# Sorting the edges of a graph layer in 50 chunks of 2,000 with one scatter each, instead of 40 chunks of 2,500 with two scatters per pair

## The reference

```python
def _L0_gnn_ref(input, edge_index, edge_attr, W_weight, W_bias):
    support = jnp.einsum('ni,oi->no', input, W_weight) + W_bias
    row, col = (edge_index[0], edge_index[1])
    messages = support[col] * edge_attr[:, None]
    output = jax.ops.segment_sum(messages, row, num_segments=N_NODES)
    return output

edge_index = jnp.stack([src, dst])
x = x + _L0_gnn_ref(_layernorm(x, axis=-1), edge_index, edge_weight, ...)
x = x + _L0_ffn_ref(_layernorm(x, axis=-1)[None], ...)[0]
```

## Time and profile before

| | |
|---|---|
| median of 3 runs | 1578.63 us (1577.52 to 1581.45) |
| profiled execution: its own time | 1581.09 us |
| profiled execution: span | 1579.2 us |
| mean granted TensorE clock | 0.942 |
| front and ranks, until the first build | 0 to 131.9 us |
| portion A, until its records are loaded back | 131.9 to 246.4 us |
| stage B, first gather to first record load | 252.8 to 588.2 us |
| records loaded and unpacked | 588.2 to 605.5 us |
| stage C | 605.5 to 1265 us |
| last LSTM steps and output | 1265 to 1579.2 us |

### The profile page before, as it was taken

How to read it: one execution, slowest core, us unless ns; L and a number is a source line. 1 busy time by engine, 2 the same in 40 slices (tenths; PEclk the granted TensorE clock), 3 DMA queues, 4 the chain that set the end, 5 groups by cost and what they waited for, 6 DMA issues and landing times.

```text
span 1579.2 us, 36191 instructions
## 1 busy us (share of the span) xinstructions
PE 1373.5 (87%) x9451; PEld 1222.1 (77%) x9451; DVE 1317.3 (83%) x4072; ACT 637.6 (40%) x2150; POOL 1028.1 (65%) x1087
## 2 busy tenths in 40 slices
PE   5688784787777876999999999999999999999990
PEld 2557783566666753899999999999999989999990
DVE  8899977999999977888888888888888655666765
ACT  0626560000000000444444444444444577777770
POOL 0325546777777777777777777777777300888883
PEclk9799886999999987999999999999999999999995
DMA  9211112333433333444444444444444343344435
GB/s 228 63 53 41 31 12 66 97 85 89 142 87 97 86 92 100 132 136 151 149 139 156 131 156 125 158 130 156 137 148 153 113 142 119 120 124 125 119 92 164
DMA packets 60867, 183.27 MB, mean 116 GB/s; under 512 B 20474, under 2 KB 22050, under 8 KB 59810
## 3 DMA queue, kind: packets, MB, share of 16 engines
q0 software_dynamic: 41312, 98.34, 22.6%
q1 hardware_dynamic: 19500, 84.30, 16.7%
HBM read 141.25 MB, written 41.17 MB: 116 GB/s over the span
## 4 chain that ended last, share of the span: by engine, by line
PE 59%; DVE 13%; issue 7%; DVEq 2%; DMA 1%; ACT 1%; POOL 1%; ACTq 0%; POOLq 0%; SPq 0%
PE bank L2020 14%; PE bank L1970 13%; PE bank L2007 10%; PE bank L2014 10%; PE bank L1922 5%; PE bank L1885 3%; DVE big_a L1233 3%; DVE big_a L1228 1%; PE bank L1980 1%; DVE big_b L1483 1%; PE bank L1989 1%; DVE big_a L1699 1%; DVE big_b L1290 1%; DVE big_c L1284 1%; PE bank L2050 1%
## 5 line engine op out<-in xcount | busy, mean ns | idle before, releaser
L633 POOL DMA_INDIRECT big_a<-support_scratch,stg_g x510 | 488.5, 958 | 159.8 <-issue 138.1
L1970 PE MATMUL bank<-big_a,big_c 128*125 128x256 f32 x1020 | 303.6, 389 | 11.1 <-DVE big_c L1567 4.3
L586 POOL DMA_INDIRECT big_a<-support_scratch,stg_g x224 | 214.3, 957 | 75.4 <-issue 56.6
L2020 PE MATMUL bank<-big_c 128*128 128x125 f32 x2048 | 256.9, 280 | 5.2 <-DVE big_c L1455 3.9
L2020 PEld LDWEIGHTS bank<-big_c 128*128 128x128 f32 x2048 | 241.3, 191 | 16.0 <-issue 7.2
L1483 DVE TENSOR_TENSOR big_b<-big_b,bank 125x256 f32 x510 | 212.2, 416 | 22.7 <-PE bank L1970 21.1
L1567 DVE TENSOR_SCALAR big_c<-consts_sb,listed 128x125 f32<-128x125 f32 x510 | 182.8, 359 | 55.5 <-PE bank L1970 46.7
L2007 PEld LDWEIGHTS bank<-xt,w_ih 128*128 128x128 f32 x1600 | 209.0, 192 | 11.3 <-ACT xt L696 0.7
L2014 PEld LDWEIGHTS bank<-big_c 128*128 128x128 f32 x1600 | 208.9, 191 | 11.2 <-ACT bank L810 0.7
L2014 PE MATMUL bank<-big_c 128*128 128x125 f32 x1600 | 209.9, 275 | 0.0
L2007 PE MATMUL bank<-xt,w_ih 128*128 128x125 f32 x1600 | 209.5, 274 | 0.5 <-ACT xt L696 0.5
(11 more groups left out here) (308 smaller groups left out, 2309.7 us busy)
## 6 DMA issues: line engine op xcount, KB each, us to landing
big_c<-gate_input_scratch SPq DMA_DIRECT2D x64, 508.0 KB, 3.5
gate_input_scratch<-pr SPq DMA_DIRECT2D x25, 1016.0 KB
big_a<-support_scratch,stg_g POOLq DMA_INDIRECT x734
support_scratch<-pr SPq DMA_DIRECT2D x12, 448.0 KB
big_b<-in_x SPq DMA_DIRECT2D x2, 1904.0 KB
out<-big_a SPq DMA_DIRECT2D x2, 1456.0 KB
big_b<-in_x SPq DMA_DIRECT2D x1, 1792.0 KB
out<-big_a SPq DMA_DIRECT2D x1, 1344.0 KB
```

The source lines that it names most:

```text
L586: pool.indirect_dma_start(out=ring[:, s, :], out_offset=None, in_=sup_d, in_offset=bass.IndirectOffsetOnAxis(ap=stg_g[:, q, j:j + 1], axis ...
L633: pool.indirect_dma_start(out=ring[:, s, :], out_offset=None, in_=sup_d, in_offset=bass.IndirectOffsetOnAxis(ap=stg_g[:, r, n:n + 1], axis ...
L1970: mm(bank[4 + POSITION[n] % PSR][0:SEGS, 0:D], oneh[:, s % HELD, 0:SEGS], ring[:, s, :], start=True, stop=True).then_inc(prod, 1)
L2020: return mm(home, w_hh[:, k, g:g + P], h_s[:, q, k, :], start=False, stop=True, skip_group_check=True)
```

## The change

A chunk is now 16 columns (2,000 edges), 50 chunks, and each has a bank and a scatter of its own: 128 blocks at most, so one group, 32 columns instead of 64 in the one-hots, 64 columns of records instead of 128. PE moves these 64 columns twice in each product (a broadcast), so that a product still moves 128 columns and writes 128 columns of PSUM, of which the first 64 are used. There are again 800 products in all (50 times 16). Portion A has 18 chunks, stage B has 232 tiles and 32 chunks; `RUN` stays 510. In portion A ACT makes the slot one-hots of every third chunk. In stage B the hardware loops are gone: the program is written out, with a chunk after every 7 tiles (`SPACING`). The masks of the front are made in 11 pieces instead of 8. Supports are spread as 25 and 3 (`RANKING, MID`) instead of 20 and 8. `rows_of_blocks` handles 5 chunks at a time, ten times, with half the elements; five of these calls fall in portion A and five in B.

```diff
-CC = 20
+CC = 16
 CHUNKS = EC // CC
-PORTIONS = (14, 26)
+PORTIONS = (18, 32)
-GRP = 2
-NPOS = GRP * BLK
-SOON, FORE, RANKING, MID = 7, 14, 20, 8
+SOON, FORE, RANKING, MID = 7, 14, 25, 3
+SPACING = 7
...
+        def chunk_at(t):
+            return t // SPACING if t % SPACING == 0 and t // SPACING < PORTIONS[1] else None
+
+        def by_scalar(k):
+            return k < K0 and k % 3 == 2
...
-            def add_blocks(m, q, rows):
-                pool.wait_ge(evac, m + 3)
-                if not isinstance(m, int) or m > 0:
-                    pool.wait_ge(scat, scattered(m))
-                pool.sem_inc(go, 1)
-                for g in range(GRP):
-                    pool.indirect_dma_start(
-                        out=rec_d, out_offset=bass.IndirectOffsetOnAxis(ap=rows(g), axis=0),
-                        in_=stg_r[:, q, g, :], in_offset=None, compute_op=ALU.add).then_inc(scat, 16)
+            def add_blocks(k, rows):
+                pool.wait_ge(evac, k + 3)
+                if k > 0:
+                    pool.wait_ge(scat, scattered(k))
+                pool.indirect_dma_start(
+                    out=rec_d, out_offset=bass.IndirectOffsetOnAxis(ap=rows, axis=0),
+                    in_=stg_r[:, k % 2, :], in_offset=None, compute_op=ALU.add).then_inc(scat, 16)
...
-            with pool.Fori(1, whole) as it:
-                for q in range(2):
-                    gather_half(0, it * 2 + q, q, HALF)
-                second_portion(it + (M0 - 1))
-            gather_half(0, whole * 2, 0, HALF)
-            second_portion(whole + M0 - 1)
-            gather_half(0, whole * 2 + 1, 1, TIL[0] - whole * RING - HALF)
+            for t in range(TIL[0]):
+                gather(t)
+                i = chunk_at(t + 1)
+                if i is not None and i >= 3:
+                    second_portion(K0 + i - 3)
+            for i in range((TIL[0]) // SPACING - 2 if TIL[0] // SPACING < PORTIONS[1] else PORTIONS[1] - 3, PORTIONS[1]):
+                second_portion(K0 + i)
             load_records(1)
...
-                V.tensor_tensor(col_h, c.broadcast_to([EP, CC, NPOS]), several(iota[0:EP, 0:NPOS], CC), ALU.is_equal
+                V.tensor_tensor(col_h, c.broadcast_to([EP, CC, BLK]), several(iota[0:EP, 0:BLK], CC), ALU.is_equal
...
-            for m in range(M0):
-                if m + 1 < M0:
-                    build(2 * m + 2, 0)
-                if m == SIDE - 2:
-                    rows_of_blocks(1)
-                copy_records(m)
-                if m + 1 < M0:
-                    build(2 * m + 3, 1)
+            for k in range(K0):
+                if k + 2 < K0:
+                    build(k + 2)
+                if k in ROWS_IN_A:
+                    rows_of_blocks(ROWS_IN_A[k])
+                copy_records(k)
...
                 for c in range(CC):
-                    ins = mm(bank[b][:, 0:2 * NPOS], slots_home(k, q)[:, c, :],
-                             col_v[:, q, c, :, :].rearrange("p v n -> p (v n)"),
-                             start=q == 0 and c == 0, stop=q == 1 and c == CC - 1)
+                    once = col_v[:, k % 2, c, :, :].rearrange("p (o v) n -> p o (v n)", o=1)
+                    ins = mm(bank[b][:, 0:4 * BLK].rearrange("p (o n) -> p o n", o=2), slots_home(k)[:, c, :],
+                             once.broadcast_to([EP, 2, 2 * BLK]), start=c == 0, stop=c == CC - 1)
```

More of the change, by code:

```diff
@@ L792, in _ @@
-            stage_rows(whole + M0 - 1)
-            act.wait_ge(prod, whole * RING + RING)
-            stage_gather(whole * RING + HALF, 1, TIL[0] - whole * RING - HALF)
+            for i in range(2):
+                stage_values(K0 + i)
+            act.wait_ge(where_r, SIDE)
+            for t in range(1, TIL[0]):
+                if t % HALF == 0 and t // HALF >= 2:
+                    stage_half(t // HALF)
+                i = chunk_at(t)
+                if i is not None:
+                    if i + 1 < PORTIONS[1] and i >= 1:
+                        stage_values(K0 + i + 1)
+                    if i >= 2:
+                        copy_records(K0 + i - 2)
+                        stage_rows(K0 + i - 2)
@@ L796, in take_input @@
+            for i in range(PORTIONS[1] - 2, PORTIONS[1]):
+                copy_records(K0 + i)
+                stage_rows(K0 + i)
             def take_input(j, q, x, free=None):
@@ L1315, in _ @@
             unpack_all(0)
-            for i in range(2, SUPERS // SIDE):
-                spread_blocks(i)
             dve.wait_ge(small_r, 1)
@@ L1336, in _ @@
                 onehot(t, t)
[L1337 to L1357 removed]
+            for t in range(TIL[0]):
+                i = chunk_at(t)
+                if i is not None:
+                    build(K0 + i)
+                    if i in ROWS_IN_B:
+                        spread_blocks(ROWS_IN_B[i])
+                        rows_of_blocks(ROWS_IN_B[i])
+                if t % HALF == 0:
+                    vals = blocks(t, HALF)
+                if t + AHEAD < TIL[0]:
+                    onehot(t + AHEAD, t + AHEAD)
+                add_tile(t, t, acc[0:SEGS, ds(vals[t % HALF], D)])
             def row_of_place(j):
```

368 lines of the change are left out of this document (152 added, 216 removed).

## The result

| | us |
|---|---|
| before, 4 runs | median 1579.25 (1577.52 to 1581.45) |
| after, 4 runs | median 1593.28 (1592.61 to 1599.71) |
| ratio after / before | 1.0087, 95% interval 1.0067 to 1.0108 |
| forecast | 1594.6, range 1583 to 1609 |

The kernel is slower by 0.87 per cent, 14 us. The profiled execution of after has a span of 1590.8 us, 11.6 more than that of before, and a granted clock of 0.94.

A forecast was written before the change was run, and what follows sets the result against it. POOL and DVE were both taken to bound stage B, PE stage C, and chains between engines portion A's later stretch. Front 0, portion A -12 and stage B +28 gave +16 us, taken to the median: 1594.6 us, range 1583 to 1609.

The forecast's parts named there:

- The bound of stage B after: Stage B: POOL (GpSimd) sets the pace at 10.8 us per chunk of 7 gathers and a scatter; chance 0.78.
- The size of stage B: Stage B: 232 gathers, 29 scatters and 3 chained scatters sum to 362.0 us against 335.4; +28 taken, bounds +26.6 and +34.
- the allowance of 1.4 us for waits on top: Stage B: +28 taken where +26.6 held without any wait inside the stage, expecting fewer waits than the 3.6 us before.
- POOL and DVE are both bounds of stage B: Stage B before the change: POOL's sum of 331.8 us and DVE's busy 322.8 of 335.4 us make both engines bounds.
- DVE's work shrinks by about 48 us ... earns nothing: Stage B: smaller builds cut DVE's work to some 275 us, but beside POOL's work this gains no time.
- Portion A: Portion A: earlier first scatter, then one chained scatter per chunk; -16 us by the rows, -12 taken, bounds -18 and -3.
- The first term: Portion A: the first eight chunks at 5.0 us each, the period worked out for both POOL and PE.
- The drawback that I held against the full 16 us: Portion A: PE partly at 1.2 GHz would add about 12 us, some absorbed, so -12 was taken instead of -16.
- Front 0, straight code 0, stage C 0: Front (bounds -2 and +2), written-out code instead of loops, and stage C each change the time by 0 us.
- Rival 1: Stage B: PE drops to 1.2 GHz under thin load and takes 12.5 us per chunk; +54, about 1649 us; chance 0.06.
- Rival 2: Stage B: without loops POOL's 0.30 us gap vanishes and DVE bounds; total -60, 1519 us; chance 0.07.
- Rival 3: Whole kernel: portion A gains 18 us, front 2, stage B costs only 24; within 5 us of no change; chance 0.09.

The follow-up runs named there:

- the tail: Changed kernel with a chunk every 6 edge tiles instead of 7 and stage B's last three scatters put between the last gathers: 1590.25 us, ratio 1.0051.

## Why the prediction was right, and where it was not

- **The bound of stage B after.** Right. GpSimd, at 1.255 us a gather and 2.02 a scatter: turns of 10.7 us (10.8 said), gaps of 0.30, no real waits outside the chain of the last three. Four runs bear the prices out: 16 scatters fewer -33.3 us, eight tiles fewer -10.3, the tail -5.7, 38.7 us more for VectorE +1.7.
- **The size of stage B.** 359.9 us against 362.0 worked out, +24.5 against the +28 taken. The sum was right to 0.6 per cent; the allowance of 1.4 us for waits on top was not needed. With the measured prices, 28.3 us were put on GpSimd: eight tiles 10.0, six scatters 12.1, the chained tail 6.2. Some 4 of them went into slack that GpSimd had before.
- **"POOL and DVE are both bounds of stage B".** Half shown. The run with 13 scatters fewer shows VectorE as a bound, at 332.9 us. That GpSimd was one too rests on a turn of 24.03 us that matched its sum; a sum that fits shows that an engine is full, not that it sets the pace. The forecast did not hang on it, since a bound of 331.8 us lies below one of 335.4 by little, and only what passes the upper one is paid.
- **"DVE's work shrinks by about 48 us ... earns nothing".** The busy time shrank by 34 us net (322.8 to 288.9), not 48. The price of a build was right: 3.93 us from start to start (3.95 said), so the builds did give back 53 us. What was left out are the operations on blocks and their rows, 5 us more by their records, and the tiles: where VectorE waits in front of an operation, its record no longer overlaps the one before, and counts in full. That the shrinking earns nothing is right as far as the sums go: with the old builds VectorE's 322.8 us, eight tiles at 0.62 and the 12.6 us in which it was idle before come to some 340 us, an estimate, still under GpSimd's 359.9. No run tried it.
- **Portion A.** From the first build to the first record load it took 102.4 us instead of 114.5, -12.1 against the -12 taken; the rows had given -16. The first scatter came at 146.96 (145.5 said) and the load 88.05 us behind it (85). The periods behind the first were 5.4 us for eight chunks (5.0 said) and 4.5 for nine (4.5 said). The first term was too small: TensorE, busy 38.9 of the 41.0 us there, needs up to 5.9 us from one permutation to the next where the broadcast of a group of rows falls in. GpSimd's own 5.0 was not it, since a bias addition took 1.3 us and not 2.63. The drawback that I held against the full 16 us, a low clock as in the earlier trace rows, did not come about: the permutations took 3.74 to 3.84 us nearly throughout. So -12 was right by luck, by two errors that cancel.
- **Front 0, straight code 0, stage C 0.** First build at 132.63 instead of 131.90: +0.7. Gaps as in the loops. From the second portion's load to the end -1.3.
- **The number.** 1593.28 us against 1594.6 is closer than the terms deserve. On the two profiled executions the change cost 11.6 us where the sum had 16, mostly since stage B grew by 24.5 and not 28. On the medians it cost 14.0, since the profiled execution of before, 1581.09 us, lies 1.8 above its median, and that of after was the fastest of its four.
- **Rival 1 (TensorE loses its clock in stage B).** It kept 0.88. At 0.79, in the run with 64 columns, stage B was as long, so the point from which the clock decides lies lower still (the prediction had put it at about two thirds of the stage at 1.2 GHz). The same mechanism was real in a place where I had not priced it as one: in portion A the doubled columns save 26 us.
- **Rival 2 (the gap shrinks).** No: 0.30 us with and without loops. **Rival 3 (A and B cancel).** No, though stage B cost 24.5 us, nearly the 24 that this rival wanted: portion A gained 12 instead of 18, and the front lost 0.7 instead of gaining 2.

What stays open: whether 96 columns would keep the clock too, what made the one chip slow, why the first scatter of A moves by up to 5 us between variants, what the kernel before does when VectorE alone is relieved, and what it does with 220 tiles in stage B.

## What to carry to other kernels

Price the engine that issues gathers and scatters by start to start, gaps that never change included, and multiply by the count: where two engines are within a few us of each other, a change that relieves one and loads the other by fourteen instructions (eight gathers and six scatters) leaves one bound, and most of those instructions are paid. To find which of two full engines sets the pace, relieve each in a run of its own and look where its time goes; relieving only one, as here, leaves open whether both were bounds. Count the spare work of each version (here the tiles) before you put a difference down to the idea. Work that TensorE does twice can cost nothing and hold its clock up, so undo such a thing alone before you call it waste.

## What the hardware showed that I had not expected

- A pass of 64 moving columns costs as much as one of 128 at the higher clock (3.69 and 3.74 us for 32, fp32, with a weight load of 128 columns for each), and with 64 columns the granted clock fell to 0.52 in a stretch in which TensorE was busy 92 per cent of the time (0.88 with 128 columns, busy 72 per cent).
- Highest busy share and bound are two things: in stage B after, VectorE is busy 80 per cent and GpSimd 76, and GpSimd is the bound. The page "Perfetto Trace Analysis" of the Trainium skill, section "Identifying the Most-Contended Engine", takes the engine with the highest occupancy and optimizes it first. Of the kernel before it names an engine that was a bound (VectorE, 96 per cent); of the changed one the run with 38.7 us more for VectorE shows that it is not.
- A scatter's issue varied in portion A of after from 1.54 to 3.54 us (the longest start at 153.83 and 213.04), in stage B it stayed at 1.6. Why is open.
